# One order on five engines: the last pair's routing chain moved between the early expert blocks, its scatters and its gate exponential on GpSimd

## The reference

```python
# layer 1: state space block, 2048 tokens, width 128, 16 heads, chunks of 64
x = layernorm(x + _L0_attn_ref(x, W_in, dt_W, dt_b, A_log, D_param, W_out, norm_w))
# layer 2: 16 experts, the best 4 of each token
dist2 = sum((x[:, :, None, :] - keys) ** 2, -1)
logits = -dist2 + einsum('bld,ed->ble', x, rw) + rb
topv, topi = top_k(logits, 4)
w = softmax(topv)
hidden = gelu(einsum('bld,efd->blef', x, w1) + b1)      # 128 -> 512
exp_out = einsum('blef,edf->bled', hidden, w2) + b2     # 512 -> 128
x = layernorm(x + sum_k w[k] * exp_out[topi[k]])
```

## Time and profile before

| | us |
|---|---|
| median of 3 runs | 317.26 (316.61 to 318.54) |
| the profiled execution | 317.52 |
| its span, first to last instruction | 315.7 |
| TensorE busy | 281.3 |
| ScalarE busy | 212.8 |
| VectorE busy | 204.6 |
| GpSimd busy | 145.4 |

### The profile page before, as it was taken

The page is one execution under the profiler, slowest core; times in us unless marked ns, Lnnn a source line. Parts: engine busy times, 40 slices in busy tenths (PEclk is TensorE's granted clock), DMA queues, the critical chain, the costliest instruction groups (busy, mean ns, idle before and its releaser), DMA issues.

```text
span 315.7 us, 10589 instructions
## 1 busy us (share of the span) xinstructions
PE 281.3 (89%) x2948; PEld 250.6 (79%) x2949; DVE 204.6 (65%) x914; ACT 212.8 (67%) x728; POOL 145.4 (46%) x145
## 2 busy tenths in 40 slices
PE   2999999999999985698889799999999999997491
PEld 2987777868778764697788699999999999996371
DVE  2138769889889897566888466565555666651172
ACT  1486467666565542676977588888888888895074
POOL 1200000756757647648377756556655565334000
PEclk9979999999999999699999999999999999999798
DMA  6999910111112113312122232222222222100794
GB/s 203 312 342 386 402 82 2 58 38 57 50 44 61 37 41 85 90 42 81 52 83 90 69 95 79 64 71 64 67 74 73 76 64 54 50 13 6 255 319 92
DMA packets 25260, 33.30 MB, mean 105 GB/s; under 512 B 4299, under 2 KB 18020, under 8 KB 24832
## 3 DMA queue, kind: packets, MB, share of 16 engines
q1 hardware_dynamic: 20432, 23.29, 24.3%
q0 software_dynamic: 4352, 8.79, 7.9%
q10 hardware_dynamic: 432, 0.67, 0.7%
HBM read 21.76 MB, written 11.50 MB: 105 GB/s over the span
## 4 chain that ended last, share of the span: by engine, by line
PE 72%; DVE 7%; DMA 7%; issue 5%; ACT 5%; POOL 1%; SPq 1%; POOLq 0%; ACTq 0%; DVEq 0%
PE bank L751 17%; PE bank L773 16%; PE bank L552 5%; PE bank L746 4%; PE bank L538 4%; PE bank L529 4%; DMA w1s<-yrows 3%; PE bank L763 3%; PE bank L577 3%; PE bank L735 3%; DMA yrows<-shared,idi 2%; PE bank L590 2%; PE bank L513 2%; DMA small<-in_small 2%; PE bank L629 2%
## 5 line engine op out<-in xcount | busy, mean ns | idle before, releaser
L1873 POOL DMA_INDIRECT yrows<-shared,idi x72 | 78.3, 1087 | 58.6 <-ACT shared L1783 30.5
L1852 POOL DMA_INDIRECT xrows<-rows_all,sli x64 | 63.8, 997 | 78.6 <-DVE sli L1108 57.5
L1762 ACT ACTIVATE shared<-bank,shared 128x128 f32<-128x128 f32 x256 | 73.2, 369 | 20.4 <-PE bank L751 19.9
L751 PE MATMUL bank<-shared 128*128 128x128 f32 x512 | 69.5, 280 | 2.7 <-issue 2.7
L773 PE MATMUL bank<-w2s,shared 128*128 x512 | 68.0, 276 | 2.5 <-DVE shared L1458 1.6
L751 PEld LDWEIGHTS bank<-shared 128*128 128x128 f32 x512 | 63.6, 195 | 4.1 <-issue 4.0
L773 PEld LDWEIGHTS bank<-w2s,shared 128*128 128x128 f32 x512 | 62.3, 192 | 2.9 <-issue 2.8
L1444 DVE COPY shared<-w1s 128x644 f32 x64 | 32.9, 514 | 27.5 <-issue 26.0
L1783 ACT ACTIVATE shared<-shared,idg 128x128 f32<-128x128 f32 x72 | 30.0, 419 | 7.6 <-DVE shared L1458 6.2
L1634 ACT ACTIVATE shared<-bank,small 128x256 f32<-128x256 f32 x64 | 25.0, 478 | 0.0
L735 PE MATMUL bank<-cst,shared 128*128 128x128 f32 x72 | 20.3, 282 | 3.7 <-ACT shared L1747 3.7
(11 more groups left out here) (222 smaller groups left out, 472.4 us busy)
## 6 DMA issues: line engine op xcount, KB each, us to landing
shared<-xrows SPq DMA_DIRECT2D x64, 70.0 KB
w1s<-in_w1T SPq DMA_DIRECT2D x1, 4128.0 KB, 24.5
w2s<-in_w2T SPq DMA_DIRECT2D x1, 4096.0 KB, 22.7
w1s<-yrows SPq DMA_DIRECT2D x8, 512.0 KB, 8.2
yrows<-shared,idi POOLq DMA_INDIRECT x72
xrows<-zrow SPq DMA_DIRECT2D x1, 1120.0 KB, 13.8
xp_all<-in_xp SPq DMA_DIRECT2D x1, 1024.0 KB, 8.5
w1s<-in_b SPq DMA_DIRECT2D x1, 1024.0 KB, 20.2
```

Source lines behind the costliest of these rows:

```text
L751: m = mm(hidden_bank(u)[:, f * P:(f + 1) * P], w[:, f * P:(f + 1) * P], xbT[u][:, :], start=True, stop=True)
L1762: m = act(hT[u][:, f * P:(f + 1) * P], hidden_bank(u)[:, f * P:(f + 1) * P], ACT.Gelu, bias=w[:, F + f:F + f + 1])
L1852: po.indirect_dma_start(out=xrows, out_offset=bass.IndirectOffsetOnAxis(ap=sli[:, g, k:k + 1], axis=0), in_=rows_all[:, g, :], in_offset=N ...
L1873: po.indirect_dma_start(out=yrows, out_offset=bass.IndirectOffsetOnAxis(ap=idi[r][:, 0:1], axis=0), in_=yw[r][:, :], in_offset=None, bound ...
```

## The change

Nothing of what is computed changes. What moves, or is done on another engine:

- TensorE: `positions(6)` goes behind the first hidden layer; `y_transpose(7)` and `out_product(7)` stand behind `hidden(1)` and ahead of the first `expert_out`; `x2_transpose(7)`, `router(7)` and `positions(7)` with `counts` go from behind blocks 6, 7 and 9 to behind blocks 2, 3 and 5; `blocks` goes from behind block 15 to behind block 10.
- VectorE: `take_w1(1)` and `ids(0)` go ahead of the last pair's `gated`; its residual, norm, logits, place and gates, and then the second table's chain (`units` to `halves`), go four to five blocks up.
- ScalarE: the copies of blocks 0 and 1 go ahead of `square(7)`, `yT_copy(7)` ahead of the first `gelu`, and `gate_exp(7)` is gone.
- GpSimd: `last_root` stands behind three scatters of pair six, the other five follow at once, then comes `last_gates`, which is new: e to the power of `gd`, with a new constant column `euler`; `gates(7)` waits for it (`ge_pool`). Only then the first four blocks' scatters. The last pair's scatters alternate with those of blocks 4 to 11, where it was 7 to 14.

```diff
@@ -142,6 +142,7 @@
     cols["part"] = p * 1.0
     cols["part_rows"] = p * float(P)
     cols["mhalf"] = np.full((P, 1), -0.5)
+    cols["euler"] = np.full((P, 1), np.e)
     cols["part64"] = p % HB * 1.0
     cols["place"] = place
     cols["rows"] = place * (P - HB * half)
@@ -362,7 +363,7 @@
         sent, sent2 = sems("sent", TOPK), sems("sent_late", TOPK)

-        cnt0_mm, c1, tb0_mm, var_dve, rv_pool = (sem(n) for n in "cnt0_mm c1 tb0_mm var_dve rv_pool".split())
+        cnt0_mm, c1, tb0_mm, var_dve, rv_pool, ge_pool = (sem(n) for n in "cnt0_mm c1 tb0_mm var_dve rv_pool ge_pool".split())

         names3 = "bt_mm h_mm yb_mm bt_act w1_dve w2_act ht_act yb_dve yw_act c_id id_dve gt_dve"
         s3 = {n: sem(n) for n in names3.split()}
@@ -800,29 +801,29 @@
             pe.wait_ge(ld["w2"], 16)
             pe.wait_ge(s1["sum_dve"], NT * NC - 1)
             rows_transpose(Step(0, 4, 0, True))
-            positions(6)
             pe.wait_ge(s1["sm0_dve"], NT)
             pe.wait_ge(s1["sm1_dve"], NT)
             moe(0)
+            positions(6)
             pe.wait_ge(s1["cb_act"], NT)
             pe.wait_ge(s1["bd_act"], NT)
-            moe(1)
+            rows_transpose(Step(0, 4, 2, True))
+            hidden(Step(0, 4, 1, True))
             y_transpose(7)
+            out_product(7)
+            expert_out(Step(0, 4, 0, True))
             moe(2)
-            out_product(7)
-            for b in range(3, 7):
-                moe(b)
             x2_transpose(7)
-            moe(7)
+            moe(3)
             router(7)
-            moe(8)
-            moe(9)
+            moe(4)
+            moe(5)
             positions(7)
             counts()
-            for b in range(10, 16):
+            for b in range(6, 11):
                 moe(b)
             blocks()
-            for b in range(16, NE):
+            for b in range(11, NE):
                 moe(b)
             pe.wait_ge(tab_done, 2)

@@ -1108,7 +1109,10 @@
                 ve.tensor_copy(sli[:, 2 * m_:2 * m_ + 2, :], slf[m_ % 2][:]).then_inc(s1["sli_dve"], 1)

             def gates(m_):
-                ve.wait_ge(s1["ge_act"], m_ + 1)
+                if m_ == NP - 1:
+                    ve.wait_ge(ge_pool, 1)
+                else:
+                    ve.wait_ge(s1["ge_act"], m_ + 1)
                 ve.tensor_reduce(gsum[m_ % 2][:], ge[m_ % 2][:], AX_X, ALU.add).then_inc(s1["gsum_dve"], 1)
                 ve.wait_ge(s1["gsum_dve"], m_ + 1)
                 ve.reciprocal(gr[m_ % 2][:], gsum[m_ % 2][:]).then_inc(s1["gr_dve"], 1)
@@ -1486,69 +1490,66 @@
             one_hot(6)
             pack_ids(6)
             chosen(6)
+            take_w1(Step(0, 4, 1, True))
             y_scale(7)
             y_add(7)
             gates(6)
             place(6)
             slots(6)
+            ids(Step(0, 4, 0, True))
             gated(7)
-            moe(0)
             moe(1)
             count_chosen(6)
-            moe(2)
-            moe(3)
             residual(7)
             res_stats(7)
             res_moments(7)
             last_var()
-            moe(4)
-            moe(5)
+            moe(2)
             normed(7)
             square_sums(7)
-            for b in range(6, 9):
-                moe(b)
+            moe(3)
             logits(7)
             best(7)
             best_ids(7)
             below_best(7)
             one_hot(7)
             chosen(7)
-            moe(9)
             count_chosen(7)
+            moe(4)
             pack_ids(7)
-            moe(10)
             place(7)
             slots(7)
+            moe(5)
             gates(7)
             units()
-            moe(11)
+            moe(6)
             shifts_of()
             floats()
             scans()
             cuts()
-            moe(12)
+            moe(7)
             owned()
             behind()
             experts()
             firsts()
-            moe(13)
+            moe(8)
             picks()
             picked()
             lows()
             ends()
-            moe(14)
+            moe(9)
             starts()
             diagonals()
-            moe(15)
-            moe(16)
+            moe(10)
+            moe(11)
             table()
             rows_of()
             row_table()
-            moe(17)
+            moe(12)
             valid()
             penalties()
             halves()
-            for b in range(18, NE - 1):
+            for b in range(13, NE - 1):
                 moe(b)
             ve.wait_ge(tab_done, 2)

@@ -1798,21 +1799,20 @@
             inv_dev(6)
             yiT_copy(15)
             x2_copy(6)
+            bt_copy(Step(0, 4, 0, True))
             gate_exp(6)
+            bt_copy(Step(0, 4, 1, True))
             square(7)
             log_ms(7)
             inv_rms(7)
             act(warm[:], ones[:, 0:1], ACT.Gelu)
-            bt_copy(Step(0, 4, 0, True))
-            moe(0)
+            yT_copy(7)
+            gelu(Step(0, 4, 0, True))
             moe(1)
-            yT_copy(7)
-            for b in range(2, 7):
+            moe(2)
+            x2_copy(7)
+            for b in range(3, 9):
                 moe(b)
-            x2_copy(7)
-            moe(7)
-            moe(8)
-            gate_exp(7)
             run_steps(ac, step3, NF - 1, 4, LO3, N3, first=9)


@@ -1879,28 +1879,32 @@
                 po.tensor_tensor(rv[(NP - 1) % 2][:], lnv[(NP - 1) % 2][:], c("mhalf").broadcast_to([P, NC]), ALU.pow
                                  ).then_inc(rv_pool, 1)

+            def last_gates():
+
+                m_ = NP - 1
+                po.wait_ge(s1["gd_dve"], m_ + 1)
+                po.wait_ge(s1["gate_dve"], m_ - 1)
+                po.tensor_tensor(ge[m_ % 2][:].rearrange("p q k -> p (q k)"), c("euler").broadcast_to([P, NC * TOPK]),
+                                 gd[m_ % 2][:].rearrange("p q k -> p (q k)"), ALU.pow).then_inc(ge_pool, 1)
+
             def moe(b):
                 give(Step(0, 4, b, True))

             ready(6)
-            for i in range(4):
+            for i in range(3):
                 send_one(6, i)
-            moe(0)
-            send_one(6, 4)
-            send_one(6, 5)
-            moe(1)
             last_root()
-            send_one(6, 6)
-            moe(2)
-            send_one(6, 7)
-            for b in range(3, 7):
+            for i in range(3, 2 * TOPK):
+                send_one(6, i)
+            last_gates()
+            for b in range(4):
                 moe(b)
             ready(7)
             for i in range(2 * TOPK):
                 send_one(7, i)
-                moe(7 + i)
-
-            run_steps(po, give, NF, 4, LO3, NBLK, first=15)
+                moe(4 + i)
+
+            run_steps(po, give, NF, 4, LO3, NBLK, first=12)

```

## The result

| | before | changed |
|---|---|---|
| median of 9 runs, us | 317.26 (315.69 to 318.61) | 315.27 (314.84 to 317.94) |
| profiled execution, us | 317.52 | 315.06 |
| its span, us | 315.7 | 313.2 |

The ratio of the times is 0.9941, with a 95% interval of 0.9913 to 0.9969: 2.0 us less between the medians (by the interval 1.0 to 2.8), inside one per cent. The forecast was 315.6.

What follows compares the result with a forecast made beforehand. TensorE, busy 281.3 of 315.7 us, bounds the kernel; only some 12.5 us of standing in the seam can be won. 2.2 less 0.5 gives 1.7; 317.52 - 1.7 = 315.8, less 0.26 for the median: 315.6, range 313.5 to 318.0.

Steps and rivals of the forecast that it cites:

- 2.2 for the seam: Between the kernel's two halves: earlier last-pair chain starts block 19's output product at 177.2 instead of 179.38, 2.2 us gained.
- 0.5 for the power: GpSimd's gate power from about 140.2 delays block 5's weight copy on VectorE; 0.5 us lost, half of 1.05.
- The power's duration: Gate exponential on GpSimd, 8 columns, estimated from the root's 0.77 us for 2 columns: 1.3 to 3.1 us.
- GpSimd in line: GpSimd's scatters after the gates: block 11's lands at 172.7, freeing block 17's output product at 173.2; TensorE wants it at 173.4.
- Rival 2: VectorE less crowded and scatters landing faster: block 19's product at 175.2, gain 4.2 us, 313.1; chance 0.16.
- The clock: TensorE at full clock in the seam; one fall costs the last pair's chain 0.6 to 1.4 us, held by the range.
- right: Seam signs: normed rows near 134, logits 138, units 146; VectorE gapless 146 to 165; no landing wait at block 19.
- wrong: Seam signs: power far over 3 us, slowed weight copy, low clock beyond 133, landing wait near block 15, dense TensorE.
- Rival 1: Chain early but power holds the weight copy fully, or clock falls twice: 316.6 to 318.0 us; chance 0.19.
- Rival 3: GpSimd's power delays block scatters and VectorE's row ids: loses from about 5 us on, 319.8 at 5 us; chance 0.07.
- Rival 4: Nothing moves as said, anywhere in the new order; no size or chance given, since the orders show each piece moved.
- the price: In the seam, TensorE stands 1.6 us for block 5's weights and 2.3 for block 6's, behind VectorE.

Runs made afterwards that it cites:

- the second chip: The unedited changed kernel run again on another chip beside the kernel before: 316.18 us, ratio 0.9958; the kernel before took 317.36 us there.
- four powers: Changed kernel plus three more 128x8 GpSimd powers behind the first, into a buffer nothing reads: 394.71 us, ratio 1.0020 to the kernel before on the third chip.

## Why the prediction was right

**The sum.** Forecast 1.7 us, from 2.2 for the seam less 0.5 for the power. Measured 2.37 behind the anchor, and 2.0 between the medians (1.2 on the second chip). That the median came within 0.3 us of the forecast is partly luck, since two medians of this kernel differ by 0.9; that the steps in the seam came in place is not. The seam's term holds: each step came where it was put, all of them 0.7 to 1.0 us early, 0.5 of which is the anchor. Forecast and measured: gated product 128.8 and 128.04, residual 131.2 and 130.37, root 133.1 and 132.17, normed rows 134.1 and 133.23, logits 137.6 and 136.60, block 5's weights 140.9 and 139.52 (end 140.02), place 143.0 and 142.29, units 146.0 and 145.18, end of the table's chain 165.0 and 164.25, block 14's hidden layer 164.9 and 164.17, block 19's output product 177.2 and 176.51. The stretch from the units on, seven steps and the chain in 17.5 us plus one step of 1.5, was forecast at 19.0 and took 19.07 (145.18 to 164.25).

**The step that was wrong** is "I take 0.5" for VectorE's copy behind the power; it was worth nothing. The power ran from 139.23 to 140.91 and block 5's copy from 139.52, and it took 0.50 us, as always. The overlap came as the forecast feared, the block did not, and four powers (above) show that this was no luck of the two starts. The row of L897, 632 for 225 ns beside a GpSimd copy, was the wrong neighbour for a power. The Trainium skill (SBUF — State Buffer, Who interferes with whom) would have had the copy stand until the power was through; the trace does not agree for this pair of instructions.

**The power's duration**, 1.3 to 3.1 from the root's row, is 1.68. The root takes 0.92 now (0.77 before), so six more columns add 0.76 us.

**GpSimd in line.** Block 3's scatter was forecast for 146.8 and started at 146.05, behind a wait of 1.36 us for its rows; pair seven's first 148.1 and 147.33; block 11's 168.4 and 168.13. Its landing was expected at 172.7 and freed block 15's ids at 171.34, after 3.2 us instead of 4.32. VectorE waited 1.44 us for it (2.62 before, at block 17), and TensorE did not: block 15's bias was done at 171.74 and the product that waits for it started at 172.72, 1.0 us of slack where 0.2 was forecast. Rival 2's premise of faster landings was thus half true, but VectorE and TensorE did not leave room to use it.

**The clock** fell once in the seam, from about 145.4 to 148.8, where block 5's output product shows 1.92 us and block 7's hidden layer 1.60. The forecast held one such fall, behind the stand at 142.4 to 144.6. It falls while TensorE follows VectorE, and so costs little at block 19: from the units to block 19's output product this kernel needs 31.33 us, and the two kernels whose profiles have no fall in that stretch, with the positions ahead and with block 6's weights ahead, 31.65 and 31.49.

**The signs.** Those for "right" came, with TensorE standing in four of the eight blocks. Two of those for "wrong" came as well and cost nothing that shows: a low clock beyond 133, and a wait for a landing at block 15, on VectorE alone.

**Rivals.** Rival 1 (the power holds the copy, or the clock falls twice) is refuted by the trace, with one fall in it, and for the power by the four powers. Rival 2 (4.2 us) failed where it was argued against: VectorE, not TensorE, sets the pace up to block 14, as the experiment with block 6's weights shows from the other side. Rival 3 needs far more than the 1.68 us. Rival 4: all pieces moved.

What the forecast did not ask is whether the stand of VectorE itself, 1.93 us before the place, had to be there. It named the price and its cause, positions behind a block that waits for weights, and took it as given. Putting six small matmuls ahead of that block returned 1.9 us between the medians, and 1.7 in the seam from the logits on.

## What to carry to other kernels

When a late chain is pulled ahead of other work on the engine that sets the pace, most of the lead is given back: here 10 us of lead for the units became 2.4 at the end. Look for the waits of that engine alone; of TensorE's 2.18 us beside it 0.56 was real, while a wait of 1.93 on VectorE, which came from small matmuls queued behind a block, was worth 1.7 to 1.9. Measure a seam from an anchor ahead of the change: with the clock falling at the same place it repeated to 0.02 us where medians differed by 0.9. Look where the clock falls and what is already late ahead of the change before a difference of one profile to another is put down to the change.

## What the runs showed of the hardware

- A GpSimd power of 128x8 takes 1.67 to 1.84 us, one of 128x2 0.73 to 0.92. VectorE's copies and additions beside it keep their durations, within 0.07 us.
- Where the granted clock falls is not fixed by the order. Changed kernel, both profiles: about 145 to 149. The kernel with the positions ahead: 131.4 to 134.8. The one with block 6's weights ahead: 123.7 to 127.1. The one with ScalarE's exponential: about 124 to 134.2. The order of all of them is the changed kernel's up to there. The last one's busy times from 125 to 130:

```profile
125.00:130.00 5.00, 4.60 (x25) 3.84 (x23) 4.24 (x18) 3.31 (x11) 2.51 (x3) 0.50 0.20 55
```

  In the changed kernel the same stretch has 2.77 us busy at a clock of 1.00. With that fall the logits are 1.6 us later (16.74 for 15.16 behind the anchor), with the one at 131.4 1.3 us, and with the one at 123.7 0.06.
- Two of the three chips need 393 us for a kernel that takes 317 on the third. A block in the dense stretch takes 1.9 us on all. The difference lies ahead of and in the seam: from 50 to 100 us, where all kernels have the same order, GpSimd is busy 17.23 us in the first chip's profile of the kernel with the positions ahead, instead of 30.05 before, and VectorE 27.64 instead of 44.65. The mean granted clock there is 0.86 instead of 1.00. The largest waits are put down to "another core or an unknown queue", up to 8.1 us a piece in the chain, though only one core is used. Some of them, of 4.3 us, begin where a block's scatter is issued (220.80 in the profile with pair seven in one run, block 4's scatter at 220.86), as a landing would; what the others are stays open.
